# Two value blocks of a decoder layer made as one pair with seven block products in place of eight, and the blocks around them reordered

## The reference

```python
# layer 0: 32 query heads, 8 key/value heads, D = 128
q = layernorm(x) @ Wq;  k = ctx @ Wk;  v = ctx @ Wv        # ctx: 1024 x 512, Wk and Wv: 512 x 1024
q, k = rotary(q), rotary(k)
x = x + tanh(g0) * (softmax(q k^T / sqrt(D) + mask) v) @ Wo
x = x + tanh(g1) * mixture_of_experts(layernorm(x))
# layer 1: the same context, q and k normalised (rms) per head instead of rotated
x = x + tanh(g2) * (softmax(q k^T / sqrt(D)) v) @ Wo1
x = x + tanh(g3) * lora_mixture(x)
```

## Time and profile before

| what | value |
|---|---|
| median of 3 runs | 1174.52 us (1174.34 to 1174.61) |
| profiled execution | 1174.92 us, its span 1172.9 us |
| granted TensorE clock | 1.00 over the span |
| busy: PE, PEld, DVE, POOL, ACT | 1164.7, 955.0, 892.1, 592.8, 452.7 us |
| matmuls | 6560 |

### The profile page before, as it was taken

One profiled execution on the slowest core, in us unless ns is written; L12 is line 12 of the kernel. 1 busy time (PEld: TensorE's weight loads), 2 busy tenths in 40 slices (PEclk: granted clock), 3 DMA queues, 4 the chain that ended last, 5 costly groups with the idle time before them and its releaser, 6 DMA issues.

```text
span 1172.9 us, 17787 instructions
## 1 busy us (share of the span) xinstructions
PE 1164.7 (99%) x6560; PEld 955.0 (81%) x6560; DVE 892.1 (76%) x1467; ACT 452.7 (39%) x860; POOL 592.8 (51%) x412
## 2 busy tenths in 40 slices
PE   9999999999999999999999999999999999999998
PEld 8888888887878888877788888777788888888776
DVE  4656546898888888889984335698888888888695
ACT  5145151322223222232453123636465454645442
POOL 5522533766667586767464112316675757536310
PEclk9999999999999999999999999999999999999999
DMA  8845635712122211211211002122203212131101
GB/s 287 274 140 169 192 132 162 271 71 81 54 77 75 89 68 58 80 45 46 99 64 37 1 1 91 59 84 79 91 1 127 80 45 81 46 127 46 37 1 72
DMA packets 57324, 106.67 MB, mean 91 GB/s; under 512 B 3632, under 2 KB 36528, under 8 KB 51888
## 3 DMA queue, kind: packets, MB, share of 16 engines
q1 hardware_dynamic: 56736, 104.82, 25.9%
q0 software_dynamic: 384, 1.05, 0.2%
q10 hardware_dynamic: 144, 0.00, 0.0%
HBM read 78.59 MB, written 27.26 MB: 90 GB/s over the span
## 4 chain that ended last, share of the span: by engine, by line
PE 92%; DVE 6%; issue 1%; ACT 0%; POOL 0%; DVEq 0%; POOLq 0%
PE ps_q L253 11%; PE ps_q L254 10%; PE ps_q L255 10%; PE ps_b L1219 8%; PE ps_b L1223 8%; PE ps_b L1220 8%; PE ps_s L1169 5%; PE ps_b L253 4%; PE ps_b L255 4%; PE ps_b L254 4%; PE ps_b L1199 4%; PE ps_s L1114 1%; PE ps_s L1115 1%; PE ps_s L1116 1%; PE ps_q L1114 1%; PE ps_q L1116 1%
## 5 line engine op out<-in xcount | busy, mean ns | idle before, releaser
L1219 PE MATMUL ps_b<-wo_hi,o_hi 128*128 128x512 f32 x440 | 171.9, 391 | 1.0 <-DVE o_lo L1891 1.0
L1220 PE MATMUL ps_b<-wo_lo,o_hi 128*128 128x512 f32 x440 | 171.2, 389 | 0.0
L1223 PE MATMUL ps_b<-wo_hi,o_lo 128*128 128x512 f32 x440 | 171.2, 389 | 0.0
L253 PE MATMUL ps_q<-hT_hi,wq_hi 128*128 128x512 f32 x384 | 152.6, 397 | 0.0
L254 PE MATMUL ps_q<-hT_lo,wq_hi 128*128 128x512 f32 x384 | 149.7, 390 | 0.0
L255 PE MATMUL ps_q<-hT_hi,wq_lo 128*128 128x512 f32 x384 | 149.5, 389 | 0.0
L1602 POOL TENSOR_TENSOR qT<-q_t 128x512 f32<-128x512 f32 x64 | 88.8, 1389 | 66.3 <-DVE q_t L1794 61.0
L1219 PEld LDWEIGHTS ps_b<-wo_hi,o_hi 128*128 128x128 f32 x440 | 82.6, 188 | 19.8 <-issue 2.9
L1223 PEld LDWEIGHTS ps_b<-wo_hi,o_lo 128*128 128x128 f32 x440 | 82.6, 188 | 17.2
L1220 PEld LDWEIGHTS ps_b<-wo_lo,o_hi 128*128 128x128 f32 x440 | 82.6, 188 | 16.8
L253 PEld LDWEIGHTS ps_q<-hT_hi,wq_hi 128*128 128x128 f32 x384 | 72.1, 188 | 18.9 <-issue 1.5
(11 more groups left out here) (363 smaller groups left out, 2954.7 us busy)
## 6 DMA issues: line engine op xcount, KB each, us to landing
wq_raw<-in_wq SPq DMA_DIRECT2D x16, 1024.0 KB, 4.7
wo_raw<-in_wo SPq DMA_DIRECT2D x16, 1024.0 KB, 5.0
kT<-kT_spill SPq DMA_DIRECT2D x32, 256.0 KB, 4.0
v_hi<-v_hi_spill SPq DMA_DIRECT2D x16, 512.0 KB, 3.7
v_lo<-v_lo_spill SPq DMA_DIRECT2D x16, 512.0 KB, 4.5
v_hi_spill<-vs_hi SPq DMA_DIRECT2D x12, 512.0 KB, 5.4
v_lo_spill<-vs_lo SPq DMA_DIRECT2D x12, 512.0 KB, 6.7
kw_raw<-in_wk SPq DMA_DIRECT2D x4, 1024.0 KB, 9.3
```

The lines of the kernel that those rows point to most:

```text
L253: nc.tensor.matmul(dst, l_hi, r_hi, start=first, stop=False)
L1219: nc.tensor.matmul(bank, o_hi[:, t, j, :], hi, start=j == 0, stop=False)
L1220: nc.tensor.matmul(bank, o_hi[:, t, j, :], lo, start=False, stop=False)
L1223: last = nc.tensor.matmul(bank, o_lo[:, t, j, :], hi, start=False, stop=j == J - 1)
```

## The change

The two value blocks of layer 0 (v00 and v01) become one pair. Context and weights are seen as 2 x 2 blocks, and the product of these is made with seven block products, each 128 tokens x 256 x 512 columns, in place of eight; sums of context blocks and of weight blocks go in, and sums of the products come out. The pair is made in four quads; a quad yields a tile of each of the four output blocks. The seven products are six matmuls each. The order becomes v10, k00, k10, pair, k01, k11, v11. Keys are transposed one tile later. The context's sums are made by POOL at the start, their low parts by POOL after block 1, the weights' sums by DVE between the key tiles of block 2, their high parts by ACT in block 2 and their low parts by POOL after them. The first layer normalisation moves: statistics to the quads, `ln_norm` of the first two tiles to the end of block 5, the rest beside block 6. In layer 1, `out_low(up, 0)` moves between the two parts of the maxima in `woven_step`, and in the step (1, 0) `att_probs_low` moves ahead of `end(1)`.

```diff
-        BLOCKS = (("v", 0, 0), ("k", 0, 0), ("v", 1, 0), ("k", 1, 0), ("v", 0, 1), ("k", 0, 1), ("k", 1, 1), ("v", 1, 1))
+        BLOCKS = (("v", 1, 0), ("k", 0, 0), ("k", 1, 0), ("v", 0, 0), ("v", 0, 1), ("k", 0, 1), ("k", 1, 1), ("v", 1, 1))
+        FIRST_OF_PAIR, SECOND_OF_PAIR = 3, 4
...
+        def kv_quad(pe, q):
...
+            if q == 0:
+                kv_split_wait(pe, FIRST_OF_PAIR)
+            bank_free(0, (c["k_staged1"], NT - 1), 4)
+            product(a, ctx(early, 0), weight(w1, 0), True, False)
+            if q == 0:
+                kv_keys_t(pe, 0, NT - 2)
+                pe.wait_ge(sums["t_lo"], 5)
+            bank_free(1, (c["k_staged1"], NT), 4)
+            product(b, ctx_sum(1), weight_sum(0), True, True)
+            if q == 0:
+                kv_keys_t(pe, 0, NT - 1)
+                pe.wait_ge(sums["t_lo"], 6)
+            bank_free(2, (c["v_lo"], NT), 5)
+            product(cc, ctx_sum(2), weight_sum(1), True, False)
+            if q == 0:
+                pe.wait_ge(c["w_lo"], 4 * FIRST_OF_PAIR + 2)
+            bank_free(3, None, 6)
+            product(d, ctx_sum(0), weight(w2, 0), True, False)
+            pe.wait_ge(sums["copied"], q + 1)
+            product(a, ctx(early, 1), weight(w1, 1), False, True)
+            if q == 0:
+                pe.wait_ge(sums["t_lo"], 7)
+            pe.wait_ge(sums["joined"], 6 * q + 2)
+            product(cc, ctx(late, 1), weight_sum(2), False, True)
+            if q == 0:
+                pe.wait_ge(c["w_lo"], 4 * SECOND_OF_PAIR)
+            pe.wait_ge(sums["joined"], 6 * q + 3)
+            product(d, ctx_sum(3), weight(w2, 1), False, True)
...
+            def quad(q):                                  # ACT
+                a = quad_banks(q)[0]
+                if q == 0:
+                    weights_hi(SECOND_OF_PAIR, (0, 1))
+                act.wait_ge(sums["product"], 7 * q + 1)
+                if q < 2:
+                    act.wait_ge(c["v_spilled"], BLOCK_SPILL)
+                else:
+                    act.wait_ge(c[f"pair_out{q % 2}"], BLOCK_SPILL * (q // 2))
+                nc.scalar.activation(vs_lo[:, quad_slot(q, 0, 1), :].bitcast(F32), a[:, :], ACT.Copy).then_inc(sums["copied"], 1)
+                if q == 0:
+                    kv_stage_keys(act, 0, NT - 2)
+                    kv_stage_keys(act, 0, NT - 1)
+                    weights_hi(SECOND_OF_PAIR, (2, 3))
+                if q == QUADS - 1:
+                    weights_hi(SECOND_OF_PAIR + 1, (0, 1))
+                pair_hi(q, 1, 1, 3)
+                act.wait_ge(sums["product"], 7 * q + 5)
+                nc.scalar.activation(vs_hi[:, quad_slot(q, 0, 0), :], a[:, :], ACT.Copy).then_inc(sums["woven_hi"], 1)
+                if q == QUADS - 1:
+                    weights_hi(SECOND_OF_PAIR + 1, (2, 3))
...
+                    if n == 2 and i == 5:                 # ACT, beside the keys of block 2
+                        weight_sum_hi(0, 7)
+                        weight_sum_hi(1, 5)
+                    if n == 2 and i == 6:
+                        weight_sum_hi(2, 8)
...
+            pool.wait_ge(sums["t_f"], 4)                  # POOL
+            keys(1)
+            context_sum_lo(0)
+            context_sum_lo(1)
+
+            context_sum_lo(2)
+            context_sum_lo(3)
+            for k in range(KC):
+                weights_lo(3, k)
+            pool.wait_ge(sums["t_f"], 8)
+            for n in range(3):
+                weight_sum_lo(n)
+
+            for k in range(2):
+                weights_lo(SECOND_OF_PAIR, k)
...
+                pair_lo(q, 1, 1, 1)
+                for k in range(2, 4):
+                    if q == QUADS - 1:
+                        weights_lo(SECOND_OF_PAIR + 1, k)
...
+                    elif n == LATE - 1:                   # DVE
+                        normed_key(cb, n, i, lambda: ln_low(dve, lns[0], i - 1) if i else None)
+                        if 0 < i < NT - 1:
+                            ln_norm(dve, lns[0], i + 1)
...
+                    if n == 2 and 2 <= i < 6:
+                        weight_sum(i - 2)
...
+                if n == 5:
...
+                    nc.vector.tensor_scalar(offset0[:, :, :, :, :], mask_i[:, :, :, :, :], 0.0, MASKED, ALU.is_equal, ALU.mult).then_inc(att[0]["masks"], 1)
+                    ln_rs(dve, lns[0], 0)
+                    ln_rs(dve, lns[0], 1)
+                    ln_norm(dve, lns[0], 0)
+                    ln_norm(dve, lns[0], 1)
...
-                maxima(us)                                # woven_step
+                part_maxima(us)
                 out_low(up, 0)
+                whole_maxima(us)
                 out_low(up, 1)
...
                         end(0)                            # second_opening
+                        att_probs_low(dve, lay, us)
                         end(1)
```

More of the change, by code:

```diff
@@ L506, in kv_sync @@
         def kv_sync(sp):
[L507 to L516, removed]
+            kv_split_wait(sp, 0)
+            kv_sync_load(sp, 2)
+            kv_sync_spill(sp, 0)
+            kv_split_wait(sp, 1)
+            kv_sync_load(sp, 3)
+            att_load_mask(sp)
+            kv_sync_spill(sp, 1)
+            kv_sync_spill(sp, 2)
+            kv_split_wait(sp, 3)
+            sp.wait_ge(att[0]["t_f"], 8)
+            kv_sync_load(sp, 5)
+            kv_split_wait(sp, 4)
+            kv_sync_load(sp, 6)
+            for q in range(QUADS):
+                kv_sync_pair(sp, q)
+            kv_split_wait(sp, 5)
+            kv_sync_load(sp, 7)
+            kv_sync_spill(sp, 5)
+            kv_split_wait(sp, 6)
+            att_load_wq(sp, 0, 0)
+            kv_sync_spill(sp, 6)
+            kv_split_wait(sp, LATE)
             att_wq_split(sp, 0, 1)
@@ L703, in weights_lo, with context_sum @@
                                         ALU.subtract).then_inc(c["w_lo"], 1)
[L705 to L719, removed]
+            def context_sum(n, x, y, op):
+                nc.gpsimd.tensor_tensor(block_sum(n)[2], x, y, op).then_inc(sums["t_f"], 1)
@@ new lines, in keys @@
+            def keys(n):
+                cb = BLOCKS[n][2]
+                for i in range(NT):
+                    g, half = divmod(i, 2)
+                    pool.wait_ge(c["k_read0"], NT * cb + i + 1)
+                    if i == 0 and cb:
+                        pool.wait_ge(c["k_spilled"], 16 * KEY_SPILLS[2 * cb])
+                    nc.gpsimd.tensor_tensor(kT_st[:, g, half * HALF:(half + 1) * HALF], k_t1[:, i % 2, :], k_t2[:, i % 2, :],
+                                            ALU.add).then_inc(c["k_staged0"], 1)
+                    if 2 <= i < 2 + KC:
+                        weights_lo(n + 1, i - 2)
@@ L720, in kv_pool @@
+            keys(5)
+            for k in range(KC):
+                weights_lo(LATE, k)
             for j in range(J):
@@ L753, in kv_dve @@
             for n in range(LATE):
                 kind, lay, cb = BLOCKS[n]
+                if n == FIRST_OF_PAIR:
+                    for q in range(QUADS):
+                        quad(q)
+                if n in (FIRST_OF_PAIR, SECOND_OF_PAIR):
+                    continue
                 if n == 1:
@@ L976, in att_sync @@
                     kv_sync_late(sp, part)
-                sp.wait_ge(kv["v_spilled"], 16 * 2 * GB * LATE_VALUES)
-                sp.wait_ge(kv["tile"], NT * len(BLOCKS))
+                pair_spilled(sp)
+                sp.wait_ge(kv["tile"], tiles_before(LATE + 1))
                 load_v(0)
```

268 lines of the change are left out of this document (211 added, 57 removed).

## The result

The changed kernel takes **1177.28 us** (median of 8 runs, 1176.94 to 1178.99) where the kernel before took 1174.57 in runs on the same chip. It is slower by 2.7 us on the medians, where "no change" (1174.5) was forecast; the ratio, taken over the means of the executions, is 1.0027, with a 95% interval of 1.0018 to 1.0036. The profiled execution took 1176.94, its span is 1175.1. So stages are compared by starts read from the traces.

A forecast was written before the change was run, and what follows sets the result against it. PE, busy 99% of the span, was taken to bound the kernel. Terms: -5.4 - 0.2 - 1.9 + 0.5 + 4.3 + 1.4 + 1.3 = 0.0, so 1174.5 us median; range 1171.0 to 1177.5, the forecast's own 1172.4 to 1176.6.

The forecast's parts named there:

- Removed: Two value blocks' 192 matmuls become 168, 5.4 us less; PE's late transposes at `ln_norm` in block 3 go, 0.2 less.
- Quad 0: Before product d PE waits for `kw_lo` of block 4, last in POOL's queue: 4.3 us more.
- 3.1 and 5.1: Quad 0's stall in us with hindrance between DVE and POOL: 3.1 if DVE always starts first, 5.1 if POOL does.
- the one with POOL first: Quad 0: POOL first at the first meeting, DVE waits 2.3, keys and `kw_hi` slip, d at 86.1: stall 5.1 us.
- Block 5: At the end of quad 3 PE waits for POOL's last low parts of block 5: 1.4 us more.
- block 6: PE's first turn of `ln_buf` waits for DVE's `ln_norm`, held up beside POOL: 1.3 us more.
- Quads 1 to 3: DVE, ACT and POOL work lies beside PE's 9.5 us per quad; no waits inside quads 1 and 2.
- the spills: Slow rival: ACT's copies in quads 2 and 3 wait for earlier quads' DMAs; at 180 GB/s 4 us, 1178.6; chance 0.10.
- Step (1, 0): Layer 1: the moved `att_probs_low` puts one `add_output` behind it, PE waits for `end(1)` and `end(3)`: 0.5 us more.
- Layer 1, "1.9 less": In steps with h = 0 PE's wait for `o_lo` at L1219 goes, as `out_low(up, 0)` comes earlier: 1.9 us less.
- the hindrance at its worst: Slow rival: DVE and POOL delays of 5.1 + 1.7 + 1.6 + 1.0 give +3.4, 1177.9 us; chance 0.10.

The follow-up runs named there:

- c2: c1 plus, in quad 0, DVE's second low part behind the second join and PE's last product waiting for `kw_lo` by chunk: 1167.94 us, ratio 0.9943.
- b1: Changed kernel with POOL's fourth `context_sum_lo` moved behind the first two `kw_lo` of block 4: 1177.31 us in one execution.
- b2: Changed kernel with the first two `kw_lo` of block 4 ahead of the third `weight_sum_lo`: first stage 180.76 us, 0.7 less, one run.
- b3: Changed kernel with PE waiting by chunk in block 5's first tile, and DVE's reciprocals and first two `ln_norm` earlier in block 5: 1173.90 us, one run.
- a4: Changed kernel with `att_probs_low` in the step (1, 0) back behind `end(1)`: 1176.66 us.
- a1: Changed kernel with `out_low(up, 0)` between the two parts of the maxima only where h = 0: 1175.91 us.
- c3: Kernel before the change, with only the swap of the maxima in the steps with h = 0: 1173.09 us, ratio 0.9989.
- b4: Changed kernel with quad 0 fed in another order, DVE making the low parts of the first and third weight sum: 1174.16 us, ratio 0.9996.
- c1: Changed kernel with a1, a4, b3 and b4 together: 1168.51 us, ratio 0.9948.

## Why the prediction was wrong, by its own steps

- **Removed, -5.4 and -0.2: right.** The count is 6536, and c2, where 0.7 of new gaps are left, shows 4.9 of it as shorter first stage.
- **Quad 0, +4.3: right in the mechanism, in part lucky in the size.** Measured 4.1 (0.6, 1.2 and 2.3). But 4.3 was a value taken between two cases, 3.1 and 5.1, and the trace shows the one with POOL first: that case was priced 1.0 too high. The row said to decide it, `weight_sum` between 1.2 and 3.5, reads 3.29, and b1 and b2 took away the two causes one at a time.
- **Block 5, +1.4, and block 6, +1.3: right.** Starts were 1.4 late beyond the usual pitch at the first (1.60 less 0.23) and 1.3 by the recorded idle time at the second. b3 removed both, and its starts against the changed kernel's give them 1.5 and 1.6.
- **Quads 1 to 3 and the spills, 0: right.** No wait of PE or for `pair_out` stands there, and the `vs_hi` spills of 256 KB landed in 3.2 us (median).
- **Step (1, 0), +0.5: right in kind, 0.6 measured**; a4 gives it back exactly.
- **Layer 1, "1.9 less": this is the step that failed.** It counted the steps with h = 0, and there it was right: against before, the lag of the changed kernel's starts shrank by 0.49, 0.55, 0.55 and 0.31 where PE enters L1517, 1.9 in all (a1 and c3, with this half alone, kept 1.7). It left out that the same two lines run in the steps with h = 1, where PE waited for no `o_lo`, and that the second reader of the moved order is POOL. `whole_maxima` came 0.6 later there and POOL's queue shifted with it; in the next step `wq_lo` was late for PE, twice also because DVE's mask add now began ahead of it. By a1 that cost 2.1 beyond the 1.7 gained (1.5 at L1412, the rest in small slips): +0.45 instead of -1.9. This one term is 2.35 of the 2.7 by which the time was missed; the others together are some 0.4 off.

Neither slow rival was the cause, the spills nor the hindrance at its worst; the time was within the range, though above the forecast's own. Two slips in the working change nothing: three tiles at 2.72 and five at 3.2 from 51.27 end at 75.4, not 75.6, and the spills at 180 GB/s come to 1178.5, not 1178.6.

## What to carry to other kernels

A line that is moved in a function runs in every phase that calls it: list for each phase who reads what now comes later, the queues of the other engines included, and not only the wait that the move is to remove. Where POOL and DVE both work from SBUF, plan their long instructions apart or let the queue in front of PE's next need be short; here a saving of 5.4 appeared only once the orders of all the feeding engines had been changed for it. Small waits at separate places added up here: -2.3, -0.6, -3.1 and -3.0 gave 1168.5, against 1168.3 expected.

## What the runs showed of the hardware

**The exclusion is for whole instructions, and who is first can change.** DVE instructions of 128x1024 with two SBUF inputs took 1.22 to 1.30 alone, and 3.29 and 3.35 when due 2.2 and 2.3 before POOL's end. The other way round, POOL's `kw_lo` took 2.05 where DVE's `weight_sum` had begun 0.3 before it (72.67, 72.99), against 1.27 alone. At 927 a shift of 0.17 between the two engines' starts decided which of them waited, and in one of the two cases PE waited as well. The Trainium skill, SBUF — State Buffer, "Who interferes with whom", has it as an exclusive lock on shared ports; all rows shown here agree.

**PE's clock fell behind one of the waits and not behind others of the same length.** In b1, after an idle of 2.18, the start-to-start pitch went from 0.23 to 0.43 for eight matmuls. Its timeline of PE, and the windows of busy time of PE, PEld, DVE, ACT and POOL (granted clock third from the end, then DMA share and GB/s):

```profile
84.22 0.56 PE L712 MATMUL ps_b<-kw_hi,hT_hi 128*128 128x512 f32 x1
84.58 0.63 PE L713 MATMUL ps_b<-kw_lo,hT_hi 128*128 128x512 f32 x1
85.00 0.63 PE L714 MATMUL ps_b<-kw_hi,hT_lo 128*128 128x512 f32 x1
```

```profile
81.00:84.00 3.00, 0.82 (x5) 0.49 (x4) 0.72 (x2) 1.49 (x3) 3.00 (x3) 1.00 0.54 204
84.00:87.60 3.60, 3.60 (x11) 2.78 (x10) 1.47 (x3) 0.63 (x1) 3.60 (x3) 0.54 0.99 315
```

A granted clock of 0.54 over that stretch is the lower of the two levels, 1.2 GHz, for nearly all of it. It cost 1.6. The changed kernel's own trace has the clock at 1.00 there, after an idle of 2.13 and with PE busy 1.44 of the three us. Such a fall would fit the two groups of executions of the kernels with the long wait, while b4, c1 and c2, which lack it, spread over 0.9 at most. The mean granted clock of the executions points the same way: 0.999 to 1.000 in the lower groups of the changed kernel and a1, 0.998 to 0.999 in the higher. But c3, which has no long wait either, had one of eleven executions 1.5 above the next, at a clock of 1.000. So that the clock is the cause of the two groups was not shown, as those executions have no trace.
